# Softmax denominators of an attention phase: from TensorE sums to a DMA-gathered tile

## The reference

```python
q, k, v = jnp.moveaxis(qkv, 2, 0)
attn = jnp.einsum('blhd,bmhd->bhlm', q, k) * HD ** (-0.5)
attn = jax.nn.softmax(attn, axis=-1)
out = jnp.einsum('bhlm,bmhd->blhd', attn, v).reshape(B, L, D)
```

## Time and profile before

| | us |
|---|---|
| median of 3 runs | 3698.73 |
| lowest and highest run | 3688.59, 3702.66 |
| span of the profiled execution (first to last instruction) | 3696.8 |
| attention, first load issued to last store issued | 880.7 to 2798.1 |

### The profile page before, as it was taken

One profiled execution on the slowest core, in us unless ns is written; L12 is line 12 of the kernel. 1 busy time (PEld: TensorE's weight loads), 2 busy tenths in 40 slices (PEclk: granted clock), 3 DMA queues, 4 the chain that ended last, 5 costly groups with the idle time before them and its releaser, 6 DMA issues. The chain is left out here.

```text
span 3696.8 us, 51173 instructions
## 1 busy us (share of the span) xinstructions
PE 3452.4 (93%) x17516; PEld 2197.3 (59%) x17516; DVE 2266.1 (61%) x3547; ACT 1552.4 (42%) x2751; POOL 1775.8 (48%) x527
## 2 busy tenths in 40 slices
PE   7899996997999999999999999999995779999999
PEld 6488885775544444444444444444434658888887
DVE  1378874444978788788788887887715932222222
ACT  0111114341166666666656666666662242222222
POOL 1033321001288788787887887877885500000000
PEclk9999998997699999999999999999997889999999
DMA  4122224446201222102222022200004641111100
GB/s 163 66 93 88 91 80 172 172 158 183 46 17 34 43 47 44 38 16 44 47 48 44 7 44 47 47 10 13 7 6 154 216 146 68 40 40 40 37 32 23
DMA packets 158137, 250.59 MB, mean 68 GB/s; under 512 B 46939, under 2 KB 68699, under 8 KB 151774
## 3 DMA queue, kind: packets, MB, share of 16 engines
q1 hardware_dynamic: 147166, 230.96, 21.1%
q10 hardware_dynamic: 10752, 16.79, 1.5%
HBM read 158.89 MB, written 88.08 MB: 67 GB/s over the span
## 5 line engine op out<-in xcount | busy, mean ns | idle before, releaser
L1147 DVE TENSOR_REDUCE att_mx<-att_pM 128x1 f32<-128x512 f32 x2048 | 1267.9, 680 | 336.2 <-PE att_pM L1213 334.0
L1104 ACT ACTIVATE att_prob<-att_pS 128x512 f32<-128x512 f32 x2048 | 1080.4, 601 | 772.8 <-PE att_pS L1261 765.2
L1083 POOL TENSOR_TENSOR att_acc<-att_acc,att_prob 128x2048 f32<-128x2048 f32 x288 | 1327.5, 4609 | 129.2 <-ACT att_prob L1104 104.1
L1213 PE MATMUL att_pM<-att_ks,att_qs 96*128 96x512 f32 x2048 | 855.1, 432 | 54.7 <-DVE att_mx L1147 33.6
L1261 PE MATMUL att_pS<-att_qs,att_ks 98*128 98x512 f32 x2048 | 868.8, 430 | 10.2 <-ACT att_prob L1104 8.0
L1261 PEld LDWEIGHTS att_pS<-att_qs,att_ks 98*128 98x128 f32 x2048 | 386.2, 190 | 555.1 <-ACT att_prob L1104 385.7
L1228 PE MATMUL att_pO<-att_prob,att_V 128*32 128x512 f32 x4096 | 548.7, 608 | 0.7 <-ACT att_prob L1104 0.7
L1213 PEld LDWEIGHTS att_pM<-att_ks,att_qs 96*128 96x128 f32 x2048 | 405.4, 198 | 200.5 <-DVE att_mx L1147 120.3
L1627 DVE TENSOR_TENSOR mlp_us<-mlp_tu,mlp_us 128x512 fp32r<-128x512 f32 x128 | 89.7, 700 | 536.0 <-ACT mlp_us L1600 536.0
L1670 PE MATMUL mlp_pu<-mlp_hs,mlp_W 128*128 128x512 f32 x1536 | 370.7, 391 | 18.9 <-DVE mlp_W L1619 18.9
L1689 PE MATMUL mlp_pa<-mlp_W,mlp_us 128*128 128x512 f32 x1536 | 368.8, 389 | 0.0
(11 more groups left out here) (181 smaller groups left out, 2984.7 us busy)
## 6 DMA issues: line engine op xcount, KB each, us to landing
qk_d<-qkv_qs SPq DMA_DIRECT2D x64, 512.0 KB, 2.7
att_qs<-qk_d SPq DMA_DIRECT2D x48, 512.0 KB, 7.4
att_ks<-qk_d SPq DMA_DIRECT2D x48, 512.0 KB, 13.8
gat_xT<-in_xT SPq DMA_DIRECT2D x32, 256.0 KB, 3.1
gat_xrow<-in_x SPq DMA_DIRECT2D x32, 256.0 KB, 2.8
x_d<-gat_x SPq DMA_DIRECT2D x32, 256.0 KB, 2.1
qkv_xr<-x_d SPq DMA_DIRECT2D x8, 1024.0 KB, 5.8
v_d<-qkv_vs SPq DMA_DIRECT2D x32, 256.0 KB, 2.0
```

What stands on the lines that cost most here:

```text
L1083: nc.gpsimd.tensor_tensor(acc[half][:], old[:], new[:], ALU.add).then_inc(added, 1)
L1104: nc.scalar.activation(prob[step % PR][:, c, :], pS[n % 3][:], ACT.Exp, scale=SCALE).then_inc(exp_done, 1)
L1147: nc.vector.tensor_reduce(mx[:, n // 4, n % 4:n % 4 + 1], bank(g, n)[:], AX.X, ALU.max).then_inc(m_read, 1)
L1213: nc.tensor.matmul(bank(g, n)[:], qs[k][0:KD, h, t * P:(t + 1) * P], ks[k][0:KD, h, mc * 512:(mc + 1) * 512], start=True, stop=True).then_ ...
```

## The change

- GpSimd adds 9 of the 16 steps of a half (eight additions). Six others (`SENT`: steps 2, 4, ..., 12) are gathered by DMA in a new tile `gathered`, 128 x 2048: SyncE issues a plain copy of the first (1 MB, SBUF to SBUF), GpSimd issues five DMAs that add to it (`accum_op=ALU.add`), each after the wait for the one before it and behind one of its own additions.
- Step 15, `gathered` and GpSimd's sum are multiplied by ones on TensorE, in one go at step FINISH = 4 of the next half, in a bank of `pS`. `pZ` is gone; `pM` has four banks.
- The reciprocals are taken on a packed tile of 128 x 16: four DMAs pack one row of each piece, VectorE inverts once, one DMA writes it to DRAM (`z_d`), four read it back over 32 partitions each. GpSimd multiplies it with the values (`scale`); SyncE issues the stores.
- The ring `prob` has eight buffers (PR 4 to 8); q and k have three (U 4 to 3). ScalarE issues the load of v at step 2 and those of q and k at steps 3, 6, 9, 12, 15, 18, for two groups ahead.
- All 16 groups are written out, with no loop.

Cut to its core (of the removed lines, which stand above, few are repeated; `place` numbers the tiles of `pM`, `turns_of` those of `pS`):

```diff
         LEAD = 6
-        EARLY = MS
-        U = 4
-        PR = 4
-        ADDED = [0, 1, 2, 4, 5, 6, 8, 9, 11, 12, 13]
+        EARLY = 4
+        U = 3
+        PR = 8
+        SENT = [2, 4, 6, 8, 10, 12]
+        LAST = MT - 1
+        ADDED = [t for t in range(LAST) if t not in SENT]
         NA = len(ADDED) - 1
-        FINISH = 2
-        INVERT = 4
-        STORE = 10
-        SUMMED = [t for t in range(MT) if t not in ADDED]
+        FINISH = 4
+        LOADS = [3, 6, 9, 12, 15, 18]
+        INVERT = 6
+        SCALED = 5
         ident = keep["ident"]
...
-        pM = [m.ps(f"pM{i}") for i in range(3)]
-        pO, pZ = m.ps("pO"), m.ps("pZ")
+        gathered = m.sb("gathered", [P, 4, 512])
+        packed = m.sb("packed", [P, 16])
+        pM = [m.ps(f"pM{i}") for i in range(4)]
+        pO = m.ps("pO")
...
+        def score_turn(what):
+            turns_of[what] = len(turns_of)
+        for g in range(NG):
+            for step in range(ST):
+                for c in range(4):
+                    score_turn((g, step, c))
+                    if c == 2 and step % MT == FINISH and (g or step >= MT):
+                        score_turn(2 * g + step // MT - 1)
+        score_turn(2 * NG - 1)
...
+        def wait_bank(pe, at):
+            if at >= 4:
+                pe.wait_ge(m_read, at - 3)
+        def load_part(eng, g, i):
+            k, at = g % U, slice(g % 2 * S, (g % 2 + 1) * S)
+            if i < 3:
+                dst, src = qs[k][i * HD:(i + 1) * HD], q_v[(0, 0, 1)[i], g // 2, :, :, at]
+            else:
+                dst, src = ks[k][(i - 3) * HD:(i - 2) * HD], k_v[(0, 1, 0)[i - 3], g // 2, :, :, at]
+            eng.dma_start(raw(dst), src).then_inc(loaded[k], 16)
+        def load_values(eng, g):
+            hp = g // 2
...
+            def send_first(n):
+                step = n % 2 * MT + SENT[0]
+                sp.wait_ge(exp_done, exps(n // 2, step))
+                if n >= 1:
+                    sp.wait_ge(exp_done, turns_of[n - 1] + 1)
+                sp.dma_start(gathered[:], prob[step % PR][:]).then_inc(first_sent, 16)
+            def reciprocals(n):
+                sp.wait_ge(exp_done, turns_of[n] + 1)
+                for c in range(4):
+                    row = rec[c * HD:c * HD + 1, :].rearrange("a (i x) -> a i x", x=16)
+                    sp.dma_start(packed[c * HD:(c + 1) * HD, :], row).then_inc(z_packed, 16)
+                sp.wait_ge(inverted, n + 1)
+                sp.dma_start(io["z_d"][n % 2].rearrange("c (i x) -> (c i) x", x=16), packed[:]).then_inc(z_kept, 16)
+                sp.wait_ge(z_kept, 16 * (n + 1))
+                for c in range(4):
+                    sp.dma_start(rec[c * HD:(c + 1) * HD, :], io["z_d"][n % 2, c:c + 1, :].to_broadcast([HD, 512])).then_inc(z_spread, 16)
...
+                    reciprocals(2 * g - 1)
+                    store(2 * g - 1)
+                else:
+                    send_first(0)
+                send_first(2 * g + 1)
+                reciprocals(2 * g)
+                if g + 1 < NG:
+                    rows(g + 1)
+                store(2 * g)
+            reciprocals(2 * NG - 1)
+            store(2 * NG - 1)
+            for x in o_stored:
+                sp.wait_ge(x, 16 * 4 * NG)
...
+            def scale(n):
+                g, half = divmod(n, 2)
+                pool.wait_ge(o_copied, n + 1)
+                pool.wait_ge(z_spread, 64 * (n + 1))
+                if g >= 1:
+                    pool.wait_ge(o_stored[half], g * 64)
+                nc.gpsimd.tensor_tensor(o[half][:], oc[:], rec[:], ALU.mult).then_inc(o_ready, 1)
+            def send(n, j):
+                step = n % 2 * MT + SENT[j]
+                pool.wait_ge(exp_done, exps(n // 2, step))
+                if j == 1:
+                    pool.wait_ge(first_sent, (n + 1) * 16)
+                else:
+                    pool.wait_ge(sent, (n * (len(SENT) - 1) + j - 1) * 16)
+                nc.gpsimd.dma_start(gathered[:], prob[step % PR][:], accum_op=ALU.add).then_inc(sent, 16)
...
+                            if n >= 1:
+                                pool.wait_ge(added, n * NA)
+                            if n >= 2:
+                                pool.wait_ge(exp_done, turns_of[n - 2] + 1)
                             old = prob[(half * MT + ADDED[0]) % PR]
                         else:
+                            pool.wait_ge(added, n * NA + i - 1)
                             old = acc[half]
                         nc.gpsimd.tensor_tensor(acc[half][:], old[:], new[:], ALU.add).then_inc(added, 1)
+                        if ADDED[i] - 1 in SENT[1:]:
...
             def free(g, step):
+                at = g * ST + step - PR
+                if at < 0:
                     return
+                act.wait_ge(step_done, at + 1)
+                t = at % MT
                 if t in ADDED:
+                    act.wait_ge(added, at // MT * NA + max(1, ADDED.index(t)))
+                elif t == SENT[0]:
+                    act.wait_ge(first_sent, (at // MT + 1) * 16)
+                elif t in SENT:
+                    act.wait_ge(sent, (at // MT * (len(SENT) - 1) + SENT.index(t)) * 16)
+                else:
+                    act.wait_ge(s_done, turns_of[at // MT] + 1)
...
             def copy_sums(n):
+                at = turns_of[n]
+                act.wait_ge(s_done, at + 1)
+                if n >= 1:
...
+            def ahead(g, step):
+                if step == 1:
+                    act.wait_ge(step_done, g * ST)
+                if step == 2 and g + 1 < NG:
+                    load_values(act, g + 1)
+                if step in LOADS and g + 2 < NG:
+                    load_part(act, g + 2, LOADS.index(step))
+            for g in range(NG):
+                for step in range(ST):
+                    n = 2 * g + step // MT - 1
+                    free(g, step)
+                    if g >= 1:
+                        ahead(g, step)
+                    for c in range(4):
+                        at = turns_of[g, step, c]
+                        act.wait_ge(s_done, at + 1)
+                        nc.scalar.activation(prob[step % PR][:, c, :], pS[at % 3][:], ACT.Exp, scale=SCALE).then_inc(exp_done, 1)
+                        if step % MT == 0 and c == 2 and n >= 0:
+                            copy(n)
+                        if step % MT == FINISH and c == 2 and n >= 0:
+                            copy_sums(n)
             copy(2 * NG - 1)
             copy_sums(2 * NG - 1)
...
+            def invert(n):
+                dve.wait_ge(z_packed, 64 * (n + 1))
+                nc.vector.reciprocal(packed[:], packed[:]).then_inc(inverted, 1)
...
+            def finish(n):
+                at = turns_of[n]
+                pe.wait_ge(exp_done, at - 2)
+                sums(pS[at % 3], prob[(n % 2 * MT + LAST) % PR], True, False)
+                pe.wait_ge(sent, (n + 1) * (len(SENT) - 1) * 16)
+                sums(pS[at % 3], gathered, False, False)
                 pe.wait_ge(added, (n + 1) * NA)
+                sums(pS[at % 3], acc[n % 2], False, True).then_inc(s_done, 1)
...
+                    for c in range(4):
+                        scores(g, step, c)
+                        if c == 2 and (g or step):
+                            behind(*divmod(g * ST + step - 1, ST))
+                            if step % MT == FINISH and (g or step >= MT):
```

More of the change, by code:

```diff
@@ L980, in attention_phase, with m_tile @@
         o_v = io["o_d"].rearrange("(g h p) (b n) -> g h p b n", h=2, p=HD, b=B)
-        def m_unit(g, step, c):
+        def m_tile(g, step, c):
             ahead = 1 if step < ST - LEAD else 2
-            return (g + ahead, (step + LEAD) % ST * MS + c) if before(g, NG - ahead) else None
-        def turn(g):
[L991 to L1014, removed]
@@ L1016, in half_before, with fill @@
-        def half_before(g, step):
-            return 2 * g + step // MT - 1
+            return (g + ahead, (step + LEAD) % ST * 4 + c) if g + ahead < NG else None
+        place = {}
+        def fill(what):
+            place[what] = len(place)
+        for q in range(NM):
+            fill((0, q))
+        for q in range(EARLY):
+            fill((1, q))
+        fill("turned 0")
+        for q in range(EARLY, LEAD * 4):
+            fill((1, q))
+        for g in range(NG):
+            for step in range(ST):
+                if step == ST - LEAD + 1 and g + 1 < NG:
+                    fill(f"turned {g + 1}")
+                for c in range(4):
+                    if m_tile(g, step, c):
+                        fill(m_tile(g, step, c))
@@ new lines, in _ @@
+            load(0)
+            load(1)
+            load_v(0)
+            load_v(1)
+            load(2)
+            rows(0)
+            for g in range(NG):
+                if g >= 1:
+                    send_first(2 * g)
+                    reciprocals(2 * g - 1)
[7 more added lines that the diff above has]
+                store(2 * g)
@@ L1194, in body @@
```

(26 more changed lines are left out.)

277 lines of the change are left out of this document (99 added, 178 removed).

## The result

The changed kernel takes 3723.58 us (median of 5, 3702.38 to 3728.21) against 3696.92 (5 runs): ratio 1.0062, 95% interval 1.004 to 1.0083. It is slightly slower. The forecast was 3605 us, clearly faster. The profiled execution is the fastest of the five, 3702.38 us with a span of 3700.6; its rows are read against that, so they explain why the kernel is not faster, and not the 20 us more of the other four. Three executions far off the rest, 3816.5 us of e2 (granted clock 0.83) and 5763 and 6637 us of the kernel before, are slow runs and left out of every comparison.

A forecast was written before the change was run, and what follows sets the result against it. TensorE was taken as the bound. A group would fall from 113.1 to 106.3 us (104.0 + 0.3 + 2.0); over 15 groups -102 us, the end +10: 3696.8 to 3605 us. Range 3560 to 3660, 8 in 10 3555 to 3830.

The forecast's parts named there:

- TensorE's floor: TensorE's matmul work in a group, with fewer sums: 104.0 us, plus 0.3 for transposing the maxima; 52.15 a half.
- VectorE: Losing four reciprocals and the product, plus a fourth maxima bank, ends the 3.9 us a group that TensorE lost.
- The packing wait: VectorE's inversion at the end of step 6 waits for four packing DMAs: nothing to 3 us a half, within the allowance.
- GpSimd: Eight additions, a product and five DMA issues at 0.4 us each: 40 us of work in a half of 52, hidden.
- The gathering chain: Serial adding DMAs, looped through ScalarE's buffer wait at step 20: 52.0 us a half, only just hidden behind TensorE.
- rival A: The chain takes TensorE's place: T of 9 gives 62.0 us a half and 3880 us, slower; chance 0.27.
- T: Time of one adding 1 MB DMA in the chain: taken as 7.0 us, between bounds of 5.2 and 10.4.
- the loads: Loads of q, k and v, about 17 us a group, delay the chain of adding DMAs by 3.4 us a half.
- rival B: Gain and chain cancel: T of 7.9 gives 56.5 us a half and 3707 us, no change; chance 0.14.
- The other way round the loop, on GpSimd: The chain's loop through GpSimd, four transfers and four additions (18.4 us), was called about as long.
- A deadline for the last DMA only: Only the fifth adding DMA was taken to hold ScalarE, before step 20, which needs the buffer of step 12.
- The end: Last group and what follows, paced by the chain: 124 us instead of 116.5, +8 to +10 us.

The follow-up runs named there:

- e2: Changed kernel with GpSimd's five adding DMAs turned into plain copies (wrong values): 3559.02 us, one run.
- e4: Changed kernel without the gathering, denominators made as before and three maxima banks, all other new paths kept: 3641.99 us, ratio 0.9833.
- e8: The no-gather version of the changed kernel, with four reciprocals of a spare tile added on VectorE each half: 3654.73 us, ratio 0.9876.
- e3: Changed kernel with ScalarE's loads of q, k and v cut to a small part, same issues (wrong values): 3605.57 us, ratio 0.9739.
- e1: Changed kernel with four adding DMAs a half instead of five, step 12 added by GpSimd instead: 3702.78 us, ratio 1.0002.
- e5: Changed kernel with four adding DMAs, sent steps three apart (1, 4, 7, 10, 13) instead of two: 3602.35 us, ratio 0.974.
- e10: Changed kernel with the six loads of q and k issued together at step 3 of a group: 3700.75 us, ratio 1.0003.
- e6: Changed kernel with three adding DMAs, sent steps 2, 5, 8, 11, and one more set of sums on TensorE: 3585.45 us, ratio 0.9698.
- e7: The no-gather version of the changed kernel, with the product of values and reciprocals back on VectorE: 3787.26 us, ratio 1.0244.

## Why the prediction was wrong

- *TensorE's floor*: right. 104.3 us a group was forecast; e2, with nothing in the way, shows 103.2.
- *VectorE*: right that the product costs the 3.9 us and the reciprocals little; e4 and e8 show 4.3 and 1.0. The packing wait cost next to nothing: VectorE waited 19 us for it from 1100 to 2600 us, and TensorE's weight loads 7 us for maxima banks.
- *GpSimd*: 0.87 us of issue instead of 0.4, 2.4 us a half. In the short distances it is hidden behind the DMA under way.
- *The gathering chain*: this step failed. It said "52.0 us: just the 52.15 of TensorE's floor" and is 55.9. ScalarE waits for the last DMA at step 4 of a half, as the prediction had it (97.5 of the 140.2 us above), so the mechanism was the right one, and so was rival A's; sizes were off. T alone is 7.3 (e3), not 7.0: the 7.5 of a second read that hides nothing was nearly exact, and I had gone below it on no row. Five times 7.3 + 0.4, and 3.5 for the loads (5 x 0.7, forecast 3.4), make 42.0 instead of 40.4. The rest, 13.9 instead of 11.6, is the way from the last landing to the next chain. At 1568.97 ScalarE resumes and at 1581.14 the next issue comes, 12.2 us; the remainder is the last DMA, which in the first half of a group lies under the loads of v and q (9.8 us from issue to resumption). Two small errors, 1.6 and 2.3 us, against a margin of 0.15. With 0.54 on the one side of such a margin I was too sure; rival B, at T = 7.9, gave 3707.
- *The other way round the loop, on GpSimd*: the prediction called it "about as long" and then left it out. In the changed kernel it is four distances, an issue and four additions, 4 x 8.42 + 0.9 + 4 x 4.7 = 53.4 us a half, also above TensorE's floor of 52.15. By the path through ScalarE e1 should win 8.4 us a half, or 2.3 with its deadline two steps earlier. Its group is no shorter: GpSimd's path is 56.1 us there, and measured are 3 x 9.0 + 29.05 = 56.0, with the 29.05 filled by additions. (The path through ScalarE, lengthened to distances of 9.0, also gives 13.9 + 6.1 + 4 x 9.0 = 56.0; this agreement is luck as far as the last distance goes, since that doesn't follow the last landing.)
- *A deadline for the last DMA only*: each sent step has its own, eight steps later. With steps 6.1 us and DMAs 8.4 us apart each is later than the one before; ScalarE's waits at steps 14 and 16 of e1 are such missed deadlines. What they cost by themselves is not measured.
- *The end*: this term failed too. 8 to 10 us more were forecast, 124 instead of 116.5. From the first exponential of the last group to the barrier it is 135.6 us instead of 115.3, 20 more. Its chains take 51 us a half (4 x 7.9 + 19.5) and not 46.8, and when ScalarE is done TensorE still waits for the last two adding DMAs:

```profile
2789.82 1.93 PE L1307 MATMUL att_pS<-att_gathered,att_ones 128*32 128x512 f32 x8 [15.34 <-DMA att_gathered<-att_prob]
```

- *The sum of the profiled execution*: the 15 groups before the last take 1677.6 us instead of 1695.5, 18 less where 102 was forecast, and the end 20 more. From the first load to the barrier that makes 1922 us instead of 1920: the two cancel.
- *The clock*: TensorE's granted clock was not in the sum. From 1100 to 2600 us it is 0.97 where TensorE is busy for 1417 of 1500 us (the changed kernel) and 1.00 where it is busy for 1466 (e5). What that cost is not measured by itself.
- *The loads*: spreading gains nothing over a burst (e10). Why the burst's median is lower by 23 us is open; so is the distance between the profiled run, 3702.38, and the other four of the changed kernel (3722.66 to 3728.21).

## What to carry to other kernels

A chain of dependent DMAs that hands back ring buffers has a rate and a deadline for each link: compare the distance of two transfers, issue and neighbours' traffic included, with the distance of the steps that feed them, not only the sum with the period. The engine that waits to issue the next one does nothing else meanwhile, so count its own work between two issues as a loop of its own, and count what is still under way when the last input is there. Here three steps apart instead of two turned 1.00 into 0.97; the best version, e6, sends less by DMA and leaves one more step to TensorE, 3585.45 us. When the forecast stands on a margin smaller than the error of its terms, the forecast is the margin, and the chances should say so.

## What the runs showed of the hardware

- A DMA of 1 MB within SBUF lands in 4.7 to 4.8 us from SyncE and GpSimd alike; adding to its target takes 7.3 alone and 8.0 beside loads. The Trainium skill, Collectives: The Full Stack, section The bandwidth ceiling, says of ReduceScatter that the add is dear for its two source reads. The trace agrees for this local add: the 2.5 us are near the 2.7 that one more read of 1 MB takes at 387 GB/s.
- The issue of an adding DMA takes 0.87 us on GpSimd, that of a plain one 0.57 (e2). The addition behind an adding one starts 0.61 us after the issue and takes 4.91 us instead of 4.58 (changed kernel, behind the issue at 1534.14).
- A VectorE product of 128 x 512 with both operands in SBUF takes 0.69 us alone, 3.06 on the mean in the kernel before and 4.6 in e7 while GpSimd adds, one of GpSimd's additions long.
- Six issues of 512 KB loads in a row block ScalarE for 7 us (e10), where one by itself takes 0.32.
